# A gated graph network over 128 graphs on one core: the first layer reassociated to adj times (x W0), layer-norm statistics as two passes on ScalarE, and the bias row added in two halves

## The reference

```python
x = _layernorm(x + L0(x))          # L0: einsum('nm,bmd->bnd', adj, x) @ weight + bias
x = _layernorm(x + L1(x))          # L1: three steps of a gated unit
# L1, with in_mat = out_mat = adj:
for _ in range(3):
    a = einsum('nm,bmd->bnd', adj, h);  av = concatenate([a, a])
    z = sigmoid(av @ w3.T + h @ u3.T + biases)
    r = sigmoid(av @ w4.T + h @ u3.T + biases)
    hv = tanh(av @ w5.T + (r * h) @ u5.T + biases)
    h = (1 - z) * h + z * hv
# _layernorm: (x - mean) / sqrt(var + 1e-5) over the 256 features
```

## Time and profile before

| | |
|---|---|
| median of 3 runs | 1619.01 us (1618.65 to 1619.64) |
| the profiled execution, its span | 1620.69 us, 1618.9 us |
| PE / PEld busy | 1599.5 us (99%) / 1348.8 us (83%) |
| DVE / ACT / POOL busy | 1427.4 (88%) / 940.4 (58%) / 265.6 us (16%) |
| DMA | 52.9% of 16 engines' span, 266.88 MB |
| chain that ended last, by engine | PE 93%, DVE 3%, DMA 1%, SPq 1% |
| mean granted TensorE clock | 0.995 of full speed |

### The profile page before, as it was taken

The page is one execution under the profiler, slowest core; times in us unless marked ns, Lnnn a source line. Parts: engine busy times, 40 slices in busy tenths (PEclk is TensorE's granted clock), DMA queues, the critical chain, the costliest instruction groups (busy, mean ns, idle before and its releaser), DMA issues.

```text
span 1618.9 us, 21710 instructions
## 1 busy us (share of the span) xinstructions
PE 1599.5 (99%) x7684; PEld 1348.8 (83%) x7684; DVE 1427.4 (88%) x1904; ACT 940.4 (58%) x1364; POOL 265.6 (16%) x302
## 2 busy tenths in 40 slices
PE   8999999999999999999999999999999999999996
PEld 8888888888888888888888888888888888888875
DVE  6788888999889998998889988999988999888888
ACT  4556556565555666565665556565656555556554
POOL 5111111111111111101111111111011111100022
PEclk9999999999999999999999999999999999999998
DMA  5444345664456553666526664355644566556534
GB/s 158 140 157 147 127 140 173 196 204 151 127 169 208 185 168 104 183 207 196 169 102 185 191 212 144 125 187 176 214 143 136 178 195 183 156 146 201 177 127 143
DMA packets 195596, 268.26 MB, mean 166 GB/s; under 512 B 18976, under 2 KB 167456, under 8 KB 195488
## 3 DMA queue, kind: packets, MB, share of 16 engines
q1 hardware_dynamic: 195488, 266.88, 52.9%
HBM read 135.21 MB, written 131.60 MB: 165 GB/s over the span
## 4 chain that ended last, share of the span: by engine, by line
PE 93%; DVE 3%; DMA 1%; SPq 1%; ACT 0%; issue 0%; POOL 0%; ACTq 0%; DVEq 0%; POOLq 0%
PE ps_r L379 46%; PE ps_h L379 31%; PE ps_a L447 8%; PE ps_l L413 5%; PE ps_l L402 3%; SPq L259 1%; DMA bias_row<-b 0%; PE ps_a L428 0%; DMA h_scratch_a<-h_blocks_a 0%; DVE out_sums L750 0%; DVE a_blocks L826 0%; DVE nat_lo L745 0%; DVE hv L866 0%; DMA a_landed<-a_scratch_b 0%; DVE h_t_h L873 0%
## 5 line engine op out<-in xcount | busy, mean ns | idle before, releaser
L826 DVE STREAM_TRANSPOSE a_blocks<-ps_a 128x512 f32<-128x512 f32 x184 | 120.0, 690 | 81.8 <-PE ps_a L447 81.5
L666 ACT ACTIVATE rh<-ps_r,bias_r 128x512 f32<-128x512 f32 x192 | 131.1, 688 | 104.2 <-PE ps_r L379 100.8
L560 ACT ACTIVATE rh_hi<-rh 128x512 fp32r<-128x512 f32 x192 | 119.0, 633 | 107.2 <-DVE rh L854 106.6
L682 ACT ACTIVATE hv<-ps_h,bias_h 128x512 f32<-128x512 f32 x192 | 128.9, 686 | 43.1 <-PE ps_h L379 42.5
L1022 POOL TENSOR_TENSOR out_var_eps_sb<-out_meanvar,eps 128x4 f32<-128x4 f32 x31 | 7.4, 239 | 808.6 <-DVE out_meanvar L756 808.6
L745 DVE TENSOR_TENSOR rh_lo<-rh,rh_hi 128x512 fp32r<-128x512 f32 x192 | 125.8, 689 | 9.2
L866 DVE TENSOR_TENSOR hv<-hv,z_sb 128x1024 f32<-128x1024 f32 x95 | 116.5, 1226 | 11.0 <-DVE hv L863 1.4
L678 ACT ACTIVATE z_sb<-ps_r,bias_z 128x512 f32<-128x512 f32 x192 | 119.9, 672 | 4.4 <-PE ps_r L379 4.4
L560 ACT ACTIVATE nat_hi<-h_landed_a 128x1024 fp32r<-128x1024 f32 x39 | 41.4, 1062 | 139.4 <-DMA h_landed_a<-h_scratch_a 129.4
L379 PE MATMUL ps_h<-rh_hi,u_hi 128*128 128x512 f32 x384 | 119.1, 391 | 1.6 <-ACT rh_hi L560 1.5
L379 PE MATMUL ps_r<-a_hi_a,w_hi 128*128 128x512 f32 x384 | 119.9, 393 | 0.6 <-ACT rh L666 0.6
(11 more groups left out here) (291 smaller groups left out, 4006.6 us busy)
## 6 DMA issues: line engine op xcount, KB each, us to landing
h_scratch_a<-h_blocks_a SPq DMA_DIRECT2D x48, 512.0 KB, 5.3
h_landed_a<-h_scratch_a SPq DMA_DIRECT2D x192, 128.0 KB, 2.9
h_scratch_b<-h_blocks_b SPq DMA_DIRECT2D x47, 512.0 KB, 3.5
h_landed_b<-h_scratch_b SPq DMA_DIRECT2D x188, 128.0 KB, 2.9
a_scratch_a<-a_blocks SPq DMA_DIRECT2D x46, 512.0 KB, 2.6
a_landed<-a_scratch_a SPq DMA_DIRECT2D x184, 128.0 KB, 2.9
a_scratch_b<-a_blocks SPq DMA_DIRECT2D x46, 512.0 KB, 2.7
a_landed<-a_scratch_b SPq DMA_DIRECT2D x184, 128.0 KB, 2.8
```

The lines of the kernel that those rows point to most:

```text
L560: return act.activation(dst, src, ACT.Copy)
L666: act.activation(rh[:, c, :], ps_r[:, c, :], ACT.Sigmoid, bias=bias_r[:, c:c + 1]).then_inc(r_ready, 1)
L682: act.activation(hv[:, c, :], ps_h[:, c, :], ACT.Tanh, bias=bias_h[:, c:c + 1]).then_inc(hv_ready, 1)
L826: tr = dve.transpose(a_blocks[:, :, c, :].rearrange("p i (b e) -> p i b e", e=Q), ps_a[:, c, :].rearrange("p (i b f) -> p i b f", b=G, f=Q))
```

## The change

For groups 4 to 31 the first layer is computed as adj (x W0). That needs x transposed: DVE's `turn` transposes its blocks, SP's `write_x` and `read_x` take them through `x_scratch` into `h_t`, ACT's `turned_high` and DVE's `turned_low` split them; `first_product` (24 matmuls of 256 columns) makes x W0 in slots `PRODUCT` = 3g - 12, `product_high` and `product_low` split that, and `graph_of_product` (6 matmuls of 512 columns) runs in `SUM` = 3g - 11. The first three groups have slots of their own (`FIRST_PRODUCTS`).

The statistics of these groups, and of the results of groups 0 to 27, leave DVE: ACT sums each row (`totals`: Identity with a summed output, four instructions), POOL makes the negative mean (`centre`), ACT sums the squared deviations (`spreads`: Square with the mean as bias and a summed output, four more), and POOL makes scale and shift. For the first layer the totals and the spreads are in slots `MEASURE` = 3g - 10 and `first_norm` in 3g - 9, now ahead of `node_high`. The bias row is added in two halves, each behind a semaphore that lets it start beside a DVE transpose. `graph_blocks` is one transpose of 1024 in place of two of 512, and `node_high` and `node_low` walk the tile in the order in which it lies.

```diff
+    FIRST_PRODUCTS = {FOUR: 2, FOUR + 1: 4, FOUR + 2: 6}
+    TURN = {g: g - FOUR if g < FOUR + 2 else STEPS * g - 16 for g in LATER}
+    PRODUCT = {g: FIRST_PRODUCTS[g] if g in FIRST_PRODUCTS else STEPS * g - 12 for g in LATER}
...
-    SUM_UP, RESULT, STORE = 1, 2, 3
+    MEAN, SPREAD, RESULT, STORE = 3, 4, 4, 5
...
+                if x_next is not None:
+                    write_x(x_next)
                 for g in output_at(s, 1):
                     read_h(nth_move[g, STEPS - 1])
                 if FOUR <= s + 1 < SLOTS:
                     read_a(s + 1)
                 if h0_next is not None:
                     read_h0(h0_next)
+                if x_next is not None:
+                    read_x(x_next)
...
-                if (g := group_at(s, GRAPH - 2)) is not None and g > FOUR:
+                if (g := group_at(s, TURN, -2)) is not None and g >= FOUR + 2:
                     load(g)
...
+            def first_product(g):
+                pe.wait_ge(y_added, after(g - 1))
+                pe.wait_ge(xt_lo_ready, g - FOUR + 1)
...
+                            mm = pe.matmul(by_node(ps_l)[:, b, :], v[:, b * C + c, :], w[:, c, :],
...
+            def graph_of_product(g):
+                pe.wait_ge(xw_lo_ready, g - FOUR + 1)
+                for half in range(C):
+                    for k, (w, v) in enumerate(((adj_hi, ax_hi), (adj_lo, ax_hi), (adj_hi, ax_lo))):
+                        mm = pe.matmul(ps_l[:, half, :], w[:, :], v[:, half, :], start=k == 0, stop=k == 2,
...
+            def totals(rows, into, ready):
+                for b in range(G):
+                    total = act.activation(rows(b), rows(b), ACT.Identity, accum_out=into[:, b:b + 1])
...
+                    spread = act.activation(squares(b), rows(b), ACT.Square, bias=neg_mean[:, b:b + 1],
+                                            scale=1.0 / 16, accum_out=into[:, b:b + 1])
...
+                if (g := group_at(s, NORM)) is not None:
+                    first_norm(g)
                 if FOUR <= s + 2 < SLOTS:
                     node_high(s + 2)
+                if (g := group_at(s, MEASURE)) is not None:
+                    first_totals(g)
+                for g in early_output_at(s, SPREAD):
+                    result_spreads(g)
                 if 2 <= s + 1 < SLOTS:
                     state_high(s + 1)
-                if (g := graph_at(s)) is not None:
-                    first_graph_high(g)
+                if (g := group_at(s, PRODUCT, -1)) is not None and g > FOUR:
+                    turned_high(g)
+                if (g := group_at(s, PRODUCT)) is not None:
+                    product_high(g)
                 if s < SLOTS:
                     reset_gate(s)
...
+                if (g := group_at(s, MEASURE)) is not None:
+                    first_spreads(g)
+                for g in early_output_at(s, MEAN):
+                    result_totals(g)
...
             def first_sum(g):
...
-                dve.wait_ge(y_added, after(g))
-                statistics(h0_norm, lambda b: rows[:, b, :], h0_stats, h0_var, g, h0_shift)
+                if g < FOUR:
+                    dve.wait_ge(y_added, after(g))
+                    statistics(h0_norm, lambda b: rows[:, b, :], h0_stats, h0_var, g, h0_shift)
...
+                for half, (produced, done) in enumerate(((a_done, s + 2), (h_ready, s))):
+                    pool.wait_ge(produced, done)
```

More of the change, by code:

```diff
@@ new lines, in product_high, with result_batch @@
+            def product_high(g):
+                act.wait_ge(xw_done, g - FOUR + 1)
+                copy(flat(ax_hi), flat(ps_l)).then_inc(xw_hi_ready, 1)
+            def result_batch(g, b):
+                return result[g % 2][:, b, :].rearrange("p (c i f) -> p c i f", c=C, f=Q)
+            def totals(rows, into, ready):
+                for b in range(G):
+                    total = act.activation(rows(b), rows(b), ACT.Identity, accum_out=into[:, b:b + 1])
+                total.then_inc(ready, 1)
@@ new lines, in spreads, with first_totals @@
+            def spreads(rows, squares, neg_mean, into, ready):
+                for b in range(G):
+                    spread = act.activation(squares(b), rows(b), ACT.Square, bias=neg_mean[:, b:b + 1],
+                                            scale=1.0 / 16, accum_out=into[:, b:b + 1])
+                spread.then_inc(ready, 1)
+            def first_totals(g):
+                act.wait_ge(y_added, after(g))
+                totals(lambda b: x_in[g % X_RING][:, b, :], x_pass[0], x_summed)
@@ L634, in node_high @@
                     src = h_landed[m % 2]
-                copy(in_quadrants(nat_hi), chunks_first(src)).then_inc(nat_hi_ready, 1)
+                copy(flat(nat_hi), flat_blocks(src)).then_inc(nat_hi_ready, 1)
             def state_high(s):
@@ L795, in first_blocks @@
                     dve.wait_ge(h0_written, g * 16)
+                if g >= FOUR:
+                    turned = [k for k in LATER if TURN[k] < BLOCKS_AT[g]]
+                    dve.wait_ge(x_written, len(turned) * 16)
                 if g < FOUR:
@@ L824, in graph_blocks @@
                     dve.wait_ge(a_written[(n - 1) % 2], ((n - 1) // 2 + 1) * 16)
-                for c in range(C):
-                    tr = dve.transpose(a_blocks[:, :, c, :].rearrange("p i (b e) -> p i b e", e=Q),
-                                       ps_a[:, c, :].rearrange("p (i b f) -> p i b f", b=G, f=Q))
+                if n == 0:
+                    dve.wait_ge(x_written, 2 * 16)
+                tr = dve.transpose(flat_blocks(a_blocks).rearrange("p (x e) -> p x e", e=Q),
+                                   flat(ps_a).rearrange("p (x f) -> p x f", f=Q))
                 tr.then_inc(a_blocks_ready, 1)
```

221 lines of the change are left out of this document (178 added, 43 removed).

## The result

| | before | changed |
|---|---|---|
| median, 6 runs each | 1619.72 us (1618.65 to 1620.09) | 1612.01 us (1610.03 to 1614.13) |
| profiled execution, span | 1620.69, 1618.9 us | 1611.77, 1610.0 us |

The ratio is 0.9951, 95% interval 0.9940 to 0.9961: about 0.5% faster, where 1633 us, 0.9% slower, was forecast. A repeat on another chip gave 1613.27 (5 runs; ratio 0.9954, 0.9941 to 0.9966). The time lies within the predicted range; the direction does not agree with the forecast.

What follows compares the result with a forecast made beforehand. PE was taken as the bound, busy 99% of the span with 93% of the chain. Span 1618.9 - 12.6 (matmuls) + 26.6 (new waits) = 1632.9, so 1633 us was forecast; 8-in-10 range 1608 to 1656 us.

Steps and rivals of the forecast that it cites:

- TensorE's work: PE's matmuls: small weight products replaced by six large ones, 0.45 us less in each of 28 groups, 12.6 us less.
- The new wait: PE waits for the reset gate's first sigmoid in slots with s mod 3 = 2: 1.4 us in 19 slots, 26.6 us.
- The landing: State's arrival for ACT's copy, 5.0 us into slots with s mod 3 = 2, bounds 4.1 to 6.0.
- The totals: ACT's four summed-output instructions ahead of the reset gate: 2.35 us taken, the upper bound; lower bound 1.22.
- rival A: Everything on ACT hides, with passes at 1.22 us and landing at 4.1; only the matmuls count: 1606 us, chance 0.13.
- Rival B: ACT's summed output is free, landing as forecast; PE waits 0.2 us in 19 slots: 1610 us, chance 0.12.
- Rival D: Matmul gain and PE's wait cancel, with a wait of 0.5 to 0.8 us: 1619 us, chance 0.07.
- The second place: z's sigmoids wanted by `state_product` after slots with s mod 3 = 2: 0.4 us late, covered by the reset gate's wait.
- DVE: Vector engine gets a little less to do and was not what PE waited for: no cost taken.
- SP and the DMAs: x's transfers delay the state's write for slots with s mod 3 = 1: costed at nothing, possibly 1.5 us in 12 slots.
- rival C: x's trips crowd the DMA queues: landing at 6.0 in 19 slots, 1 us waits in 12 others: 1663 us, chance 0.10.
- Start and end: Kernel's start loses 0 to 3 us to x's transfers, its end regains 0 to 2: zero for both together.

Runs made afterwards that it cites:

- experiment 1: Changed kernel with the first layer's totals made twice, the second pass right behind the first: 1638.30 us, ratio 1.0102 to the kernel before.
- experiment 2: Changed kernel with the load of x back in slots with s mod 3 = 1, ahead of the state's write: 1633.97 us, ratio 1.0088.
- experiment 3: Changed kernel with the first layer's totals moved behind the reset gate (after `reset_high`): 1617.58 us, ratio 0.9985 to the kernel before.
- experiment 4: Changed kernel with the edit of experiment 3 and the results' normalisation of groups 0 to 26 at the front of the next slot: 1615.85 us, ratio 0.9973.
- experiment 7: Kernel before with only the statistics of the results of groups 0 to 27 moved to ACT: 1633.84 us, ratio 1.0083.
- experiment 6: Changed kernel with the edit of experiment 5 and the results' normalisation (groups 0 to 26) behind z and the candidate's first half: 1605.36 us, ratio 0.9909.
- experiment 8: Changed kernel with the statistics of both normalisations back on DVE, the reassociated product kept: 1675.67 us, ratio 1.0340 to the kernel before.
- experiment 5: Changed kernel with totals and `turned_high` ahead of `node_high` in slots with s mod 3 = 2 from slot 8 on: 1607.69 us, ratio 0.9920.
- experiment 9: Changed kernel with the bias row added in one operation behind the graph product instead of two halves: 1622.45 us, ratio 1.0014 to the kernel before.

## Why the prediction was wrong, and where it was right

**TensorE's work** was right: 280 matmul rows less, 12.1 us less busy where 12.6 was worked out (0.44 us a group, not 0.45), 2.87 and 1.36 us for the two products, all of it on the path.

**The new wait was right in its mechanism and wrong in its size, and this term turned the sign.** The step that failed is "`r_ready` at 5.0 + 5.9 = 10.9. PE wants it at ... 9.52". Measured in slot 17 it is 9.47 (between 8.27 and 10.28 over the 18 regular slots of this kind), and two of its parts are off, both to the same side:

- *The landing*, 5.0 forecast. Over the 18 regular slots of this kind it is between 3.14 and 5.15, 4.0 in the middle; the bounds given were 4.1 to 6.0. In slot 17 it is 4.33. The read goes out at 313.64, +16.45 from slot 16's start where "+16.8 to +17.0" stood (+15.9 in the middle of the 18), for two reasons. "The residual add, for which it also waits" does not gate it: in all 18 slots that add ends after the read has gone. And without a load ahead the write takes 4.72 us until the read, not 5.97, which more than makes up for its being issued 0.6 us later than before. The gate was read from a semaphore's name (`res_added`) without asking which group's add it counts. The rows of before could have told: the add ended at +15.56 and the read went at +16.96, so the add was 1.4 us early and something else, the write, was what the read waited for. Then the data came 4.2 us after the read, below the 4.3 to 4.95 taken.
- *The totals*, 2.35 forecast, 1.60 measured. I took the upper bound of 1.22 to 2.35, on the argument that a summed output spoils the overlap. It does not: in the trace the sum is fetched by an instruction of its own, and the next activation starts 0.40 us after the last, 0.09 more than in a plain copy.

Together 0.7 + 0.75 us in slot 17, of a wait of 1.4. What is left is the one slot where the landing is at 5.00 (slot 26; in the three others at 4.8 to 5.15 a wait for z at the slot's start had already moved PE by 0.5 to 0.8). Experiments 1 and 2 each add some 1.8 us, to the passes or to the landing, about what both parts together were off by, and each gives the forecast waits (18 and 17 of them in regular slots) and nearly the forecast time (1638 and 1634). That shows the path and the wait; that either size alone would have done it is not shown. With two bounds open on one margin the number of slots with a wait jumps from 18 to 1 within 1.8 us; the forecast took the pessimistic end of one and the upper half of the other. The case that came true in the regular slots is nearest to rival A, which had 0.13: a landing at 4.0 (its 4.1) and totals near the lower bound, `r_ready` at 4.0 + 5.1 = 9.1 (its 8.9), and the gate hidden in 17 of 18 slots. Rival B's 1610 us is the nearest time, but by luck: its 0.2 us in each of 19 slots did not come, and its landing was a microsecond late. Rival D, a wait of 0.5 to 0.8 us in every slot, did not come either.

**The second place** (z at the end of a slot with s mod 3 = 2), 0.4 us "covered" by the first wait, costs nothing in the changed kernel: no slot with s mod 3 = 0 is longer than its matmuls need. It costs in experiments 3 and 4 (4.9 and 9.2 us). What remains in the changed kernel is a third place that the prediction had not worked out: z at the end of slots with s mod 3 = 1, behind the results' normalisation, 2.9 us in five waits. It is also what costs in experiment 7, and experiments 4 and 6 remove it.

**DVE** at nothing: the text said what the cover was, PE's 14.96 us a slot; experiment 8 shows it is thin, and that the two halves of the change need each other. "A little less to do" was right for the change, but hid that it would cost some 62 us if the statistics stayed on DVE.

**The bias halves** at nothing: right for the change as made. The whole add in the place of the halves costs 9 us, and beside the halves DVE is nearly at its old speed (`hv - h` 1.37 us in the slots with s mod 3 = 0, 1.18 before). The text did not see that the alternative had a price.

**SP and the DMAs**: no wait for `rh` in slots with s mod 3 = 1, as forecast; the queue went from 52.9% to 59.0%, and rival C did not come.

**Start and end** at zero: -1.4 +1.2 and -3.6 us. Of the start the 1.4 is within what the same start takes from kernel to kernel. For the end the forecast named the right cause, `bn_stats` gone from the DVE chain (experiment 7 has the gain too), and bounded it at 2; it was 3.6. The four `bn_stats` and `bn_aggr` of group 27 take 1.8 us in the trace of before (1542.83 to 1544.64); where the other 1.8 comes from was not followed. Without these 5.0 us at both ends the span would be 3.9 us shorter and not 8.9.

**Rival A** needed passes at 1.22 us and a landing at 4.1; the passes are 1.60, and the landing is even earlier in half of the slots. It had no waits for z, which together with slots 86 and 91 keep the changed kernel from its time; 1606 us is what experiments 5 and 6 reach (1607.69 and 1605.36) by taking the passes out of the gap between landing and gate and the normalisation from in front of z.

## What to carry to other kernels

When an in-order engine waits for a landing and then does new work ahead of something that PE needs, the forecast hangs on a margin of tenths, so work out both ends as a number of slots that wait, and do not choose an end; check which condition of a wait was really last by comparing its time with the issue in the trace. One slot is not enough for a margin of tenths: slot 17 was at the early end of the landings in experiment 2 and had the second shortest write before. Put new work ahead of the wait, into the idle time, not behind it: the same totals and copy cost 4 us less there. A DMA that leaves the queue in front of a critical write can be worth more than the matmuls that the change is about.

## What the runs showed of the hardware that was not expected

- A summed output of ACT shows as an instruction of its own, `ACTIVATION_READ_ACCUMULATOR`, 0.19 us, behind each activation. Four activations of 128x256 with one take 1.60 us (318.81 to 320.41) in place of 1.22, so 0.09 more each, and the squared deviations, with one pointer operand, 1.97 (325.83 to 327.80).
- 512 KB from SBUF to the scratch take 4.9 us in the middle of 18 slots (3.9 to 5.8) until the read behind them can go, and 6.3 us (5.0 to 7.1) with a 512 KB load issued 0.5 us ahead on the same queue (experiment 2; 6.5 in the kernel before).
- DVE's two-input operation on 128x1024 takes 1.18 us alone and 2.67 when it starts 0.82 us after a 2.40 us add of POOL: it ends 1.09 us behind POOL's end (experiment 9).
- A late semaphore costs PE some 0.3 us more than the idle time of its matmul, because the weight load ahead of it waits too (0.92 against 0.50 us in slot 26), and 0.2 to 0.3 us in slots where the matmul shows no wait at all (experiment 3).
- Waits of PE of some 3 us are followed by a stretch at the lower clock: 0.50 from 384.80 to 387.60 behind 3.21 us (experiment 8).
